# A two-part change at the start of an adaptive-norm block: block 1's convolution tail by channel groups, and six weight splits moved from VectorE to GpSimd

## The reference, cut to what matters

```python
# sub-layer 1: gated state-space mixer over the whole sequence (INNER = 384, S = 16, 3 taps)
h    = layernorm(modulated x) * ln_w + ln_b
proj = h @ W_in;  data, gate = proj[..., :384], proj[..., 384:]
conv = sum(xp[:, j:j + seq, :] * conv_w[:, j] for j in range(3))     # causal, by channel
u    = silu(conv)                                                    # conv * sigmoid(conv)
Bu   = einsum('bti,si->tbs', u, Bm)
state_t = state_{t-1} @ (I + A.T) + Bu_t                             # scan over 4096 steps
out  = sigmoid(gate) * (states @ Cm.T) @ W_out;  x = x + ga * (h + out)
# sub-layer 2: 16 experts, C = 256 -> q, k, v of H = 128 each
logits = normed(x) @ normed(sim) - sigmoid(gates)
w      = softmax over the active experts (or the two best, if none is active)
q, k, v = sum_e w[:, e] * (x @ proj[e]) ;  full attention; sum_e w[:, e] * (o @ o_proj[e])
```

## Time and profile before

| | |
|---|---|
| median of 3 runs | 1417.59 us (1417.49 to 1417.81) |
| profiled execution | 1418.72 us, of which the instructions span 1416.8 us |
| mean granted TensorE clock of the profiled execution | 0.989 |
| TensorE busy | 97% of the span |
| VectorE busy | 81% |
| GpSimd busy | 50% |
| ScalarE busy | 48% |

### The profile page before, as it was taken

How to read it: one execution, slowest core, us unless ns; L and a number is a source line. 1 busy time by engine, 2 the same in 40 slices (tenths; PEclk the granted TensorE clock), 3 DMA queues, 4 the chain that set the end, 5 groups by cost and what they waited for, 6 DMA issues and landing times. The chain is left out here.

```text
span 1416.8 us, 21192 instructions
## 1 busy us (share of the span) xinstructions
PE 1373.8 (97%) x7050; PEld 1220.9 (86%) x7050; DVE 1153.7 (81%) x2192; ACT 675.7 (48%) x1347; POOL 706.2 (50%) x636
## 2 busy tenths in 40 slices
PE   6989999999999999999999899999999999999997
PEld 5879999999999999999999777878787878878776
DVE  7887786777858768686678698989898999999866
ACT  5611402103022130130101398888888888888983
POOL 2421301313013121130123287888888888989897
PEclk9989999999999999999999899999999999999999
DMA  9101011100111001100138410000001000000000
GB/s 264 42 15 29 20 38 37 31 27 27 40 31 40 28 27 40 31 25 23 53 105 267 148 61 16 16 30 16 31 10 37 8 23 23 16 31 16 10 14 30
DMA packets 83133, 62.96 MB, mean 44 GB/s; under 512 B 13984, under 2 KB 75856, under 8 KB 82768
## 3 DMA queue, kind: packets, MB, share of 16 engines
q1 hardware_dynamic: 54880, 45.94, 10.3%
q10 hardware_dynamic: 28144, 15.67, 3.7%
HBM read 36.55 MB, written 25.03 MB: 43 GB/s over the span
## 5 line engine op out<-in xcount | busy, mean ns | idle before, releaser
L1741 PE MATMUL ps<-w_hi,memory_r 128*128 128x384 f32 x2048 | 565.5, 342 | 0.0
L1442 DVE SCALAR_TENSOR_TENSOR wst<-ps,w_cur,wst 128x384 f32<-128x384 f32 x480 | 295.1, 615 | 164.4 <-PE ps L1741 152.4
L1962 POOL TENSOR_TENSOR memory_rest<-memory_rest,pf 128x512 f32<-128x512 f32 x248 | 345.8, 1394 | 68.5 <-ACT pf L2069 60.4
L1741 PEld LDWEIGHTS ps<-w_hi,memory_r 128*128 128x128 f32 x2048 | 374.9, 189 | 3.4 <-issue 1.4
L1741 PE MATMUL ps<-w_lo,memory_r 128*128 128x384 f32 x1024 | 344.0, 336 | 0.0
L2135 DVE TENSOR_TENSOR p_lo<-pf,p_hi 128x512 fp32r<-128x512 f32 x256 | 282.1, 1102 | 36.0 <-ACT p_hi L2071 35.0
L1741 PEld LDWEIGHTS ps<-w_lo,memory_r 128*128 128x128 f32 x1024 | 193.3, 189 | 4.7 <-issue 1.4
L2069 ACT ACTIVATE pf<-ps 128x512 f32<-128x512 f32 x256 | 153.1, 598 | 72.8 <-PE ps L2241 54.8
L2029 ACT COPY ps<-shift_rows 128x512 f32<-128x512 f32 x254 | 151.7, 597 | 5.8
L2071 ACT ACTIVATE p_hi<-ps 128x512 fp32r<-128x512 f32 x256 | 152.1, 594 | 0.0
L2116 DVE TENSOR_REDUCE mx<-ps 128x1 f32<-128x512 f32 x224 | 147.6, 678 | 1.2 <-PE ps L2230 1.2
(11 more groups left out here) (256 smaller groups left out, 2211.2 us busy)
## 6 DMA issues: line engine op xcount, KB each, us to landing
qk_scratch<-wst ACTq DMA_DIRECT2D x56, 128.0 KB, 2.2
x_scratch<-memory SPq DMA_DIRECT2D x8, 512.0 KB, 2.9
o_scratch<-memory_rest SPq DMA_DIRECT2D x16, 256.0 KB, 3.2
x2b<-x_scratch SPq DMA_DIRECT2D x32, 128.0 KB, 2.2
out_x<-memory_rest SPq DMA_DIRECT2D x32, 128.0 KB, 1.7
v_scratch<-wst ACTq DMA_DIRECT2D x60, 64.0 KB, 1.8
memory<-in_x SPq DMA_DIRECT2D x7, 512.0 KB, 4.0
memory_r<-qk_scratch SPq DMA_DIRECT2D x9, 256.0 KB, 4.6
```

Source lines behind the costliest of these rows:

```text
L1442: nc.vector.scalar_tensor_tensor(out=dst, in0=src, scalar=w, in1=dst, op0=ALU.mult, op1=ALU.add).then_inc(moe_acc, 1)
L1741: ins = nc.tensor.matmul(ps[:, s % MOE_BANKS, 0:H3], x_part[p][:, k, rows], w_part[:, k, e].rearrange("p t h -> p (t h)"), start=(k == 0 a ...
L1962: nc.gpsimd.tensor_tensor(p_sum[:, p], p_sum[:, p], pf[:, j % PB], ALU.add).then_inc(p_summed, 1)
```

## The change

Block 1's convolution, sigmoid and u are made by channel groups, with the functions that block 0 already uses (`first_conv`, `first_sigmoid`, `first_u`), and TensorE's three parts of B u for block 1 stand together behind step 3, each waiting for its own group. VectorE splits experts 8 and 9 before the slot, and GpSimd splits experts 10 to 15, behind block 0's routing and ahead of the low part of the input and `residual(0, 1)`; VectorE splits nothing in the slot. The counters of the convolution grow by two more, which the waits further on follow.

```diff
-        LATE_SPLIT, FIRST_BU = 8, 1
+        LATE_SPLIT, FIRST_BU = 10, 3
-        CONV_MORE, X2_MORE, DVE_B_MORE = FI - 1, TT - 1, 2 * (TT - 1)
+        CONV_MORE, X2_MORE, DVE_B_MORE = 2 * (FI - 1), TT - 1, 2 * (TT - 1)
...
@@ gpsimd, before the slots
                 pool.wait_ge(h2t_ready, 1)
                 pool.wait_ge(h2t_first, 1)
-                pool.wait_ge(u_ready, FI + 1)
+                pool.wait_ge(dve_b, DVE_B + DVE_B_MORE)
+                pool.wait_ge(w_lo_ready, LATE_SPLIT)
+                for n in range(LATE_SPLIT, E):
+                    pool.wait_ge(w_hi_ready, n + 1)
+                    nc.gpsimd.tensor_tensor(w_lo[:, :, n], w_raw[:, :, n], w_hi[:, :, n].bitcast(F32), ALU.subtract
+                                            ).then_inc(w_lo_ready, 1)
                 rest = slice(P, BT)
                 nc.gpsimd.tensor_tensor(xt_lo[0][:, :, rest], h2t[:, :, rest], xt_hi[0][:, :, rest].bitcast(F32),
                                         ALU.subtract).then_inc(xlo_ready, 1)
...
@@ scalar, before the slots
                 first_squares(2, TT).then_inc(sumsq_ready, 1)
+                first_sigmoid(0, 1)
                 evacuate_projection(FI, FI + 1, 0, 1)
-                evacuate_projection(FI + 1, FI + 2, 0, 1)
+                first_sigmoid(1, 1)
                 act.wait_ge(proj_mm, 4 * FI)
                 nc.scalar.copy(xt_hi[0], first_src).then_inc(h2t_ready, 1)
-                evacuate_projection(FI + 2, 2 * FI, 0, 1)
-                conv_sigmoid(0, 1)
+                first_sigmoid(2, 1)
+                evacuate_projection(FI + 1, 2 * FI, 0, 1)
                 exp(0, 0)
...
@@ vector, before the slots
                 ins.then_inc(dve_const, 1)
+                split_w(8, 9)
                 more.block(0, 0)
...
                 first_h2(3)
-                for n in range(TAPS - 1):
-                    conv_piece(n, 0, 1)
+                split_w(9, LATE_SPLIT)
+                first_conv(0, 1)
+                first_conv(1, 1)
+                first_u(0, 1)
+                first_conv(2, 1)
                 dve.wait_ge(h2t_ready, 1)
                 tt(xt_lo[0][:, :, 0:P], h2t[:, :, 0:P], xt_hi[0][:, :, 0:P].bitcast(F32), ALU.subtract
                    ).then_inc(xlo_first, 1)
+                first_u(1, 1)
                 for n in range(ROUTE_PIECES - 1):
                     route_piece(n, 0, 0)
-                dve.wait_ge(csig_ready, 1 + FI)
-                tt(sg, sg, cv, ALU.mult).then_inc(u_ready, 1)
+                first_u(2, 1)
...
@@ vector, in the slot
-                        if is_first(i, p) and LATE_SPLIT + s < E:
-                            split_w(LATE_SPLIT + s, LATE_SPLIT + s + 1)
...
-                        if is_first(i, p) and s == FIRST_BU + FI - 1:
+                        if is_first(i, p) and s == FIRST_BU:
                             take_input(0, 1, BU_BANK1)
...
@@ tensor
-                    pe.wait_ge(u_ready, 1 + f if not p else 1 + FI)
+                    pe.wait_ge(u_ready, p * FI + f + 1)
...
-                        if is_first(i, p) and FIRST_BU <= s < FIRST_BU + FI:
-                            if s == FIRST_BU:
-                                pe.wait_ge(proj_evac, 2 * FI + FI + 1)
-                            first_input_term(s - FIRST_BU, 0, 1, BU_BANK1)
+                        if is_first(i, p) and s == FIRST_BU:
+                            pe.wait_ge(proj_evac, 2 * FI + FI + 1)
+                            for f in range(FI):
+                                first_input_term(f, 0, 1, BU_BANK1)
```

More of the change, by code:

```diff
@@ L506, in slot @@
                     if ahead == 1:
-                        sp.wait_ge(u_ready, NB + FI - 1)
+                        sp.wait_ge(u_ready, NB + CONV_MORE)
                         for n in range(3):
@@ L750, in data_out @@
                 def data_out(i, p):
-                    act.wait_ge(conv_ready, past(i, p, 1, 0, CONV_MORE))
-                    act.wait_ge(u_ready, past(i, p, 1, 0, CONV_MORE))
+                    done = upto(i, p, 1, 0) + CONV_MORE if i else FI
+                    act.wait_ge(conv_ready, done)
+                    act.wait_ge(u_ready, done)
                     nc.scalar.copy(data[:, :, 0:TAPS - 1], data[:, :, BT:BT + TAPS - 1]).then_inc(halo_ready, 1)
@@ L872, in _, with first_sigmoid @@
                     "p (f j) -> p f j", f=FI), 0.0)
-                def first_sigmoid(f):
+                def first_sigmoid(f, p=0):
                     if f == 0:
-                        act.wait_ge(ht_lo_ready, 1)
-                    act.wait_ge(conv_ready, f + 1)
+                        act.wait_ge(ht_lo_ready, p + 1)
+                        wait(act, bu_mm, p)
+                    act.wait_ge(conv_ready, p * FI + f + 1)
                     nc.scalar.activation(sg[:, f], cv[:, f], ACT.Sigmoid).then_inc(csig_ready, 1)
@@ L969, in slot @@
                         act.wait_ge(w_ready, NB)
-                        act.wait_ge(u_ready, NB + FI - 1)
+                        act.wait_ge(u_ready, NB + CONV_MORE)
                         act.wait_ge(bu_mm, NB)
@@ L1245, in pow_copy, with first_conv @@
                     nc.vector.tensor_copy(powers_t[:, k % 2], ps[:, QK_BANK, P:2 * P]).then_inc(pow_ready, 1)
-                def first_conv(f):
-                    dve.wait_ge(proj_evac, f + 1)
+                def first_conv(f, p=0):
+                    dve.wait_ge(proj_evac, p * 2 * FI + f + 1)
                     for j in range(TAPS - 1):
                         if j:
-                            dve.wait_ge(conv_link, f + 1)
+                            dve.wait_ge(conv_link, p * FI + f + 1)
                         ins = nc.vector.scalar_tensor_tensor(out=cv[:, f], in0=data[:, f, j:j + BT],
@@ L1333, in _, with first_u @@
                 split_w(0, 1)
-                def first_u(f):
-                    dve.wait_ge(csig_ready, f + 1)
+                def first_u(f, p=0):
+                    dve.wait_ge(csig_ready, p * FI + f + 1)
                     tt(sg[:, f], sg[:, f], cv[:, f], ALU.mult).then_inc(u_ready, 1)
```

## The result

The changed kernel takes 1424.21 us (1422.05 to 1424.96, 5 runs), 6.6 us more than before (1417.59; five runs now, 1415.22 to 1417.81); the ratio to before is 1.0049, interval 1.0037 to 1.006. It is slower, as forecast, but by about twice the 3.4 us of the forecast and just outside the range of 1418.0 to 1424.0.

What follows compares the result with a forecast made beforehand. TensorE, busy 97% of the span, bounds the kernel; a restart 0.7 us later at scan product 2 plus 2.7 us lost to slow clock gave +3.4 us, 1421.0 us on the median 1417.59; 8-in-10 range 1418.0 to 1424.0.

Steps and rivals of the forecast that it cites:

- The step that failed: At scan product 2, TensorE, held by the late load of block 2's x, restarts 0.7 us later than 103.73.
- The second term: Behind TensorE's wait at scan product 2: 0.50 clock for 5.4 us, half lost, +2.7 us (bounds 0 and 5.9).
- The split of expert 8: On VectorE, 0.95 us, put into the wait for TensorE's first output; the copy at 71.62 stays (bounds 0, +0.3 us).
- The faster one: Block 2's x load does not hold VectorE; scan product 2 at 92.0 instead of 103.73; 1405.9 us; chance 0.09.
- No measurable change: Same wait at scan product 2, clock back in under 4.3 us or restart earlier; +0.7 to 2.8 us; chance 0.28.
- Slower by much: Behind the wait at scan product 2, clock down 11.8 us, 5.9 us lost; +6.6 us, 1424.2; chance 0.10.
- the three signs: Wrong if L994 starts before 99 us, GpSimd instructions take well under 1.7 us, or clock recovers within 2 us of restart.

Runs made afterwards that it cites:

- Experiments 1: The changed kernel with GpSimd doing residual(0, 1) ahead of its six splits: 1412.90 us, ratio 0.9971 to the kernel before.
- 9: The changed kernel with VectorE's five norm pieces of block 2 moved behind later steps in the first slot: 1414.35 us, ratio 0.9985 to before.
- its control: The kernel before with VectorE's five norm pieces of block 2 moved behind later steps in the first slot: 1423.89 us, ratio 1.0053.
- Experiment 4: The changed kernel with 50 unread matmuls filling TensorE's 13.35 us wait ahead of scan product 2: 1419.72 us, ratio 1.0021 to before.
- The second trace: The kernel before, run again without any edit: 1416.85 us, ratio 0.9997.
- experiment 7: The kernel before with 21 unread matmuls filling TensorE's 5.44 us stall ahead of block 1's B u: 1415.74 us, ratio 0.9998.
- second trace of the change: The changed kernel, run again without any edit: 1424.23 us, ratio 1.0046 to before.
- Experiment 8: The changed kernel with the split of expert 8 moved behind block 0's last h2 instruction, next to expert 9's: 1424.18 us, ratio 1.0049 to before.
- experiment 12: The changed kernel with residual(0, 1) ahead of GpSimd's six splits and VectorE's norm pieces of block 2 behind later steps: 1408.39 us, ratio 0.9944 to before.
- part 2 alone: The kernel before with two early VectorE splits and six on GpSimd, convolution and B u as before: 1423.69 us, ratio 1.0053.
- part 1 alone: The changed kernel with experts 8 to 15 split on VectorE in the slot again, none on GpSimd: 1415.65 us, ratio 0.9995 to before.

## Why the prediction was right in kind and short in size

**Right.** No stall at the start, B u as one run of 5.46 us (5.5 forecast), step 4 at 83.57 (83.3), the end of step 10 at 92.2 (92.0). GpSimd: the six splits and the low part 12.8 us from 80.5 (12.3 from 80.0), the residual 2.34 + 0.17 + 2.34 (4.9), the load asked for at 98.1 (97.2) and landed at 102.2 (101.2), VectorE's wait 13.63 us (13), TensorE's 13.35 (12.4), the slow clock behind the restart 4.9 us (5.4). Experiments 1 and 9 with its control show from two sides, the load made early and the load let be but not waited for, that this wait is the loss. That step 4 came out so near is partly luck: step 0 began at 74.01, 0.87 us later than before, and the four steps took 4.3 us where I had allowed 4.7.

**The step that failed** is "restart is at 101.2 + 0.1 + 3.1 = 104.4 us, 0.7 us later than before". Experiment 4, which takes the slow clock away and leaves the restart late, measures 3.0 us (1.7 to 4.3) for this term. Both ends of the 0.7 were off.

The "before" in it was the 103.73 of one execution, in which the clock came back late, and the time of the forecast was then put on the median of the others. That execution took 1418.72 us, more than each of the five runs that the result compares with. I had written that work in this stretch costs its double and that TensorE waits for VectorE at the end of it, and did not ask which of the two sets the 103.73. The second trace puts scan product 2 at 34.7 us behind the transposes instead of 37.4, and experiment 7 puts it at 33.6 at full clock. Against 38.2 to 38.3 in the change, the restart is 3.5 us later than in the second trace of before, and 0.9 later than in the first. Two traces do not tell where the median execution lies between them.

The 104.4 was 1.2 us too early, for the restart came at 105.57: GpSimd started 0.5 us later than forecast, its seven instructions took 0.4 us more (1.83 us from one to the next where the row had 1.76), and the load and the way from it to the restart 0.1 us more each.

**The second term**, the clock, was right in mechanism and, by the traces, in size: 2.7 us in the sum, 2.3 and 2.8 in the two traces of the change (3.5 to 4.0 by the times of experiment 4, which are less sharp). The two together are 5.3 to 7.0 us, against 6.5 to 6.9 measured. In the first pair of traces the error is hardly seen: there scan product 2 is 1.84 us later and scan product 4 is 4.11 us later than before, of which 0.8 us is won back by the end. The slow stretches at the attention's start, where before was slow from 799 to 809 us and the change for less, can be the reason.

**The split of expert 8** was costed at nothing, for it would go into a wait. In the first trace of the change that wait was not there. The VectorE instructions ahead of the split took 2.16 us beside one of GpSimd's (0.25 us for the same two in before) and ended at 58.3; the split followed, and the first x2 instruction came at 59.11, against this row of before:

```profile
58.22 0.42 DVE L1262 TENSOR_TENSOR memory<-memory,ps 128x256 f32<-128x256 f32 x1 [1.49 <-PE ps L1620]
```

The transposes follow 8.1 us behind it in both, at 67.23 and 66.37, so about 0.9 us was lost at the start, where the forecast had "the copy stays where it is (bounds: 0 and +0.3 us)"; that copy came at 72.48 instead of 71.62. The routing moved with it, and so did GpSimd's start. In the second trace of the change VectorE did wait for TensorE there, and the split cost little. Experiment 8 met such a start too, so that the 0.9 us is read from the rows of one trace and not tested.

**The rivals.** The faster one was wrong for this kernel (the load did hold VectorE), but its price was good: 11.7 us of lead, of which experiment 12 keeps 9. "No measurable change" asked for the clock back in under 4.3 us; it took 4.9 and 6 us. "Slower by much" was my case for a long slow stretch, at 1424.2; the time is that, its cause is not: the stretch behind the restart was 4.9 us in one trace and 6 us in the other, not 11.8. None of the three signs that I had named for a wrong prediction came up, because all three looked at the changed kernel, and the greater error was in the number for the kernel before.

## What to carry to other kernels

Before work is given to an engine that looks idle, read what stands behind it in that engine's list and who waits for the last of it: here a buffer was freed 9 us later, a load went with it, and one waiting instruction in VectorE's list turned 9 us that could be won (experiment 12) into 7 lost; putting the release first was a change of order only. And a sum made on one profiled execution should be checked for terms that vary between executions, above all a stretch at half clock: find out whether it lies on the path (fill the wait and see whether the time falls) before its end is used as "the time before". A second trace of the kernel before would have shown it.

## What the runs showed of the hardware

The same 5.45 us wait of TensorE was followed by 6 us at half clock in one execution and by 12 us in another, with the same instructions. A wait of 2.88 us (part 2 alone) was also followed by a stretch at half clock, which began only behind the restart at 106.21: the granted clock was 0.96 from 106 to 107 us and 0.50 from 107 to 110. But 6.23 us of wait (part 1 alone) had TensorE back at full clock under 4 us behind the restart at 91.71. In these traces the length of the wait does not tell the length of the slow stretch.

Two engines that both read SBUF with two inputs stretch each other: on VectorE a 0.95 us split to 2.6 us and a 1.66 us group of four instructions to 4.90 us, on GpSimd the two residual instructions from 2.34 us each to 3.07 and 2.87 beside such splits. A small VectorE copy with one input was stretched too (L1202 of before, 0.18 us; the same copy took 1.26 us beside GpSimd's splits in the change), while the accumulations, with one input in PSUM and one in SBUF, kept their 0.61 us.
